# An attention output projection in three rounded products instead of one float32 product, and one turn later in TensorE's order

## The reference

```python
q = (x @ Wq + bq).reshape(B, N, H, d).transpose(0, 2, 1, 3)      # N = 164, H = 12, d = 16
k = (x @ Wk + bk).reshape(B, N, H, d).transpose(0, 2, 1, 3)
v = (x @ Wv + bv).reshape(B, N, H, d).transpose(0, 2, 1, 3)
scores = jnp.einsum('bhqd,bhkd->bhqk', q, k) * SCALE
allowed = jnp.abs(idx[:, None] - idx[None, :]) <= 64
attn = jax.nn.softmax(jnp.where(allowed[None, None], scores, -jnp.inf), axis=-1)
out = jnp.einsum('bhqk,bhkd->bhqd', attn, v).transpose(0, 2, 1, 3).reshape(B, N, D)
return out @ Wo + bo                                               # the product that is changed
```

## Time and profile before

| | us |
|---|---|
| median of 3 runs | 2368.55 |
| lowest, highest | 2356.19, 2369.52 |
| the profiled execution | 2377.01 |
| its span, first to last instruction | 2375.3 |
| TensorE busy | 2272.5 (96%) |
| VectorE busy | 1870.8 (79%) |
| ScalarE busy | 1412.7 (59%) |
| GpSimd busy | 297.8 (13%) |
| mean granted clock of TensorE | 0.98 |

### The profile page before, as it was taken

One profiled execution on the slowest core, in us unless ns is written; L12 is line 12 of the kernel. 1 busy time (PEld: TensorE's weight loads), 2 busy tenths in 40 slices (PEclk: granted clock), 3 DMA queues, 4 the chain that ended last, 5 costly groups with the idle time before them and its releaser, 6 DMA issues.

```text
span 2375.3 us, 49109 instructions
## 1 busy us (share of the span) xinstructions
PE 2272.5 (96%) x20033; PEld 2123.1 (89%) x20033; DVE 1870.8 (79%) x2241; ACT 1412.7 (59%) x1391; POOL 297.8 (13%) x169
## 2 busy tenths in 40 slices
PE   6599989999999889999999999999999999999999
PEld 5266778888888779999999999999999999999999
DVE  7599765666666578676676776679999999999996
ACT  6389403444444463543533534588998888888881
POOL 7522100000000013232232231000000000000000
PEclk9799998999999889999999999999999999999999
DMA  6555240111111101111111111120000000000000
GB/s 209 163 153 151 75 161 28 47 46 47 47 47 47 44 27 34 54 46 45 51 46 51 45 49 36 57 92 24 26 28 23 23 23 23 23 23 23 23 19 10
DMA packets 115454, 129.98 MB, mean 55 GB/s; under 512 B 17063, under 2 KB 106167, under 8 KB 115127
## 3 DMA queue, kind: packets, MB, share of 16 engines
q1 hardware_dynamic: 95215, 103.54, 14.5%
q10 hardware_dynamic: 16520, 14.34, 2.0%
q0 software_dynamic: 3616, 10.54, 1.7%
HBM read 92.79 MB, written 35.58 MB: 54 GB/s over the span
## 4 chain that ended last, share of the span: by engine, by line
PE 62%; DVE 2%; ACT 0%; issue 0%; DVEq 0%
PE spline_acc L1988 17%; PE spline_acc L1984 10%; PE spline_acc L1956 10%; PE spline_acc L1958 10%; PE spline_acc L1957 10%; PE spline_acc L1985 5%; PE spline_xT L764 0%; DVE spline_f L1726 0%; DVE spline_f_high L1726 0%; DVE spline_f_low L1726 0%; DVE spline_weights_split L1762 0%; DVE spline_b L1732 0%; DVE spline_front L1732 0%; DVE spline_f L1715 0%; DVE spline_front L803 0%; DVE spline_b L803 0%
## 5 line engine op out<-in xcount | busy, mean ns | idle before, releaser
L1956 PE MATMUL spline_acc<-spline_f,spline_weights_high 128*128 128x328 f32 x1536 | 483.2, 315 | 2.5 <-DVE spline_weights_low L1698 2.5
L1957 PE MATMUL spline_acc<-spline_f,spline_weights_high 128*128 128x328 f32 x1536 | 480.9, 313 | 0.0
L1958 PE MATMUL spline_acc<-spline_f,spline_weights_low 128*128 128x328 f32 x1536 | 480.6, 313 | 0.0
L1988 PE MATMUL spline_acc<-spline_weights,spline_f 128*128 128x192 f32 x1968 | 342.5, 327 | 0.0
L1988 PEld LDWEIGHTS spline_acc<-spline_weights,spline_f 128*128 128x128 f32 x1968 | 316.6, 190 | 0.0
L1984 PE MATMUL spline_acc<-spline_weights_split,spline_f_high 128*128 128x384 f32 x984 | 304.9, 374 | 2.1 <-DVE spline_f L1726 2.1
L1956 PEld LDWEIGHTS spline_acc<-spline_f,spline_weights_high 128*128 128x128 f32 x1536 | 289.1, 188 | 2.8 <-DVE spline_weights_low L1698 2.8
L1958 PEld LDWEIGHTS spline_acc<-spline_f,spline_weights_low 128*128 128x128 f32 x1536 | 290.2, 189 | 0.0
L1957 PEld LDWEIGHTS spline_acc<-spline_f,spline_weights_high 128*128 128x128 f32 x1536 | 289.7, 189 | 0.0
L1985 PE MATMUL spline_acc<-spline_weights_split,spline_f_low 128*128 128x192 f32 x984 | 248.5, 253 | 0.0
L1715 DVE SCALAR_TENSOR_TENSOR spline_f<-spline_front 128x984 fp32r<-128x984 f32 x128 | 148.6, 1202 | 93.7 <-PE spline_acc L1958 88.3
(11 more groups left out here) (240 smaller groups left out, 4932.3 us busy)
## 6 DMA issues: line engine op xcount, KB each, us to landing
spline_front<-pos_scr SPq DMA_DIRECT2D x32, 540.0 KB, 4.3
hid_scr<-spline_hid SPq DMA_DIRECT2D x64, 164.0 KB, 1.8
spline_xn<-hid_scr SPq DMA_DIRECT2D x41, 256.0 KB, 3.1
attend_spread<-rec_scr SPq DMA_DIRECT2D x128, 61.5 KB, 2.2
pix_scr<-spline_front SPq DMA_DIRECT2D x32, 225.0 KB
spline_weights_raw<-w SPq DMA_DIRECT2D x1, 6144.0 KB, 21.6
spline_step_to<-w SPq DMA_DIRECT2D x36, 128.0 KB, 2.1
spline_step_from<-w SPq DMA_DIRECT2D x36, 128.0 KB, 2.1
```

The costliest lines, as they stand in the source:

```text
L1956: nc.tensor.matmul(z, high, x_high, start=start, stop=False)
L1957: nc.tensor.matmul(z, high, x_low, start=False, stop=False)
L1958: last = nc.tensor.matmul(z, low, x_high, start=False, stop=stop)
L1988: last = nc.tensor.matmul(z, rest[:, cols], w2[:, i, r - SETS, :], start=False, stop=stop)
```

## The change

- `project_out` becomes 18 matmuls in F32R: for each head group high x high, high x low, low x high, of the weighed sums (`oT_high`, `oT_low`) and the output weights (`wo_high`, `wo_low`).
- The weights are split once, ahead of pair 0: ScalarE rounds, VectorE subtracts, and TensorE waits for both (`wo_ready`). Raw `wo` is loaded into the buffer of a later result.
- VectorE forms the product of `weigh` twice, once rounded into `oT_high`, once in full over `mixed`. A new step, `low_o`, subtracts; it, and no longer `weigh`, tells TensorE that the sums are there (`weighed`). It stands in turn 0 behind the maximum and, in the second sequence, behind the layer norm's statistics.
- TensorE projects after turn 1 instead of turn 0, and VectorE's residual rows move to turn 1, too.
- `spread` and `oT_low` share memory, `rec` moves into a free part of another buffer.

```diff
@@ buffers @@
-        wo, wo_in = sb("attend_wo", [P, HG, D]), sem("attend_wo_in")
+        wo_high, wo_low = (sb(f"attend_wo_{k}", [P, HG, D], F32R) for k in ("high", "low"))
+        wo_in, wo_ready = sem("attend_wo_in"), sem("attend_wo_ready")
...
-        rec = [sb(f"attend_rec{i}", [P, PART]) for i in range(2)]
-        spread = [sb(f"attend_spread{i}", [P, SC]) for i in range(2)]
-        oT = [sb(f"attend_oT{i}", [P, HG, TOK]) for i in range(2)]
+        rec = [c.rows[:, i, 64:64 + PART] for i in range(2)]
+        spread, oT_low = share(nc, stack, [(f"attend_spread{i}", [P, SC], F32) for i in range(2)],
+                               [(f"attend_oT_low{i}", [P, HG, TOK], F32R) for i in range(2)])
+        oT_high = [sb(f"attend_oT_high{i}", [P, HG, TOK], F32R) for i in range(2)]
         h2 = [sb(f"attend_h{u}", [P, 4, D]) for u in range(2)]
+        wo = h2[1][:, 0:HG, :]
@@ VectorE @@
             def weigh(t, i):
 
                 dve.wait_ge(spread_in[i], 64 * t + 64)
-                nc.vector.tensor_tensor(oT[i][:].rearrange("p g n -> p (g n)"), mixed[i][:], spread[i][:],
-                                        ALU.mult).then_inc(weighed, 1)
+                nc.vector.tensor_tensor(oT_high[i][:].rearrange("p g n -> p (g n)"), mixed[i][:], spread[i][:],
+                                        ALU.mult).then_inc(weigh_step, 1)
+                nc.vector.tensor_tensor(mixed[i][:], mixed[i][:], spread[i][:], ALU.mult).then_inc(weigh_step, 1)
+
+            def low_o(t, i):
+
+                dve.wait_ge(weigh_step, 4 * t + 2 * i + 2)
+                nc.vector.tensor_tensor(oT_low[i][:].rearrange("p g n -> p (g n)"), mixed[i][:],
+                                        oT_high[i][:].bitcast(F32).rearrange("p g n -> p (g n)"),
+                                        ALU.subtract).then_inc(weighed, 1)
...
                         if q == 0 and not first:
+                            low_o(t - 1, i)
+                        if q == 1 and not first:
                             residual(tt - 1 if u == 0 else tt, v, i, use(t, (Y_LAST if last else Y)[i]))
...
             norm_out(0, 1, start(START["X"][1]))
+            dve.wait_ge(wo_ready, 1)
+            nc.vector.tensor_tensor(wo_low[:], wo, wo_high[:].bitcast(F32), ALU.subtract).then_inc(wo_ready, 1)
             pair(0, 0, first=True)
...
             weigh(PAIRS - 1, 0)
+            low_o(PAIRS - 1, 0)
...
             weigh(PAIRS - 1, 1)
+            low_o(PAIRS - 1, 1)
@@ ScalarE @@
             high(mh[:], start(START["MAX"]))
+            act.wait_ge(wo_in, 16)
+            nc.scalar.activation(wo_high[:], wo, ACT.Copy).then_inc(wo_ready, 1)
             pair(0, 0, first=True)
@@ TensorE @@
                     for g in range(HG):
-                        last = nc.tensor.matmul(xb[0:ROWS, bank, n * D:(n + 1) * D],
-                                                oT[i][:, g, n * ROWS:(n + 1) * ROWS],
-                                                wo[:, g, :], start=(g == 0), stop=(g == HG - 1))
+                        y, cols = xb[0:ROWS, bank, n * D:(n + 1) * D], slice(n * ROWS, (n + 1) * ROWS)
+                        nc.tensor.matmul(y, oT_high[i][:, g, cols], wo_high[:, g, :], start=(g == 0), stop=False)
+                        nc.tensor.matmul(y, oT_high[i][:, g, cols], wo_low[:, g, :], start=False, stop=False)
+                        last = nc.tensor.matmul(y, oT_low[i][:, g, cols], wo_high[:, g, :], start=False,
+                                                stop=(g == HG - 1))
...
-                        if q == 0 and not first:
+                        if q == 1 and not first:
                             project_out(a - 2, i, use(t, Y[i]))
...
-            pe.wait_ge(wo_in, 16)
+            pe.wait_ge(wo_ready, 2)
             pair(0, 0, first=True)
```

More of the change, by code:

```diff
@@ L873, in attend_phase @@
         mix_ready, inverted, weighed = sem("attend_mix_ready"), sem("attend_inverted"), sem("attend_weighed")
+        weigh_step = sem("attend_weigh_step")
         h_ready = sem("attend_h_ready")
@@ L923, in _ @@
                 load(sp, x[u], x_in[u], u)
-            sp.dma_start(wo[:], a["wo"]).then_inc(wo_in, 16)
+            sp.dma_start(wo, a["wo"]).then_inc(wo_in, 16)
             sp.dma_start(w_raw[:], a["w1"].rearrange("p i (h r) o -> p (i h) (r o)", h=2)).then_inc(w1_in, 16)
```

## The result

The changed kernel took **2510.48 us** (median of 4 runs, 2485 to 2515) against 2367.11 before (4 runs, 2356 to 2370): **1.0587** times, 95% interval 1.0549 to 1.0625. The profiled execution took 2506.89 us, its span was 2505.2 at a mean granted clock of 0.939; before these were 2375.3 and 0.98. I predicted 2550 in a range of 2415 to 2625.

The account below looks back on a forecast made before the run. TensorE sets the attention loop's pace. New waits, start and end add 58 us to the profiled 2377.0, 2426 against the median; clock falls add 128, giving 2554, stated as 2550, range 2415 to 2625.

Parts of the forecast that it names:

- The projection as cover: In turn 0 the projection lies over VectorE's 1.07 us maximum, which turn 1's scores need; moved, it no longer covers it.
- The four waits: TensorE's new idle: first sequence 1.25 us before turn 1, 0.45 at transposes; second 0.75 before turn 1, 1.6 before projection.
- The projection at 1.76: 18 rounded matmuls take 1.76 us, scaled from ten in 1.05; some 0.25 less on average, 8 us in 32 sequences.
- The rival that its weight loads show: In the projection no weight load hides: 4 us more in 31 places, 2550 us; chance 0.02.
- Start and end: Before the loop TensorE waits for the split output weights, +4.9, taken as 7; the last two sequences add 2.4 us.
- The clock: TensorE's clock falls to 1.2 GHz in the loop's new waits, one and a half falls a pair: 128 us.
- They still land in time: Loads of the spread reciprocals still arrive before VectorE's product, though second product and reciprocal are 0.6 us late at most.

Follow-up runs that it names:

- with fillers: The changed kernel with dense filler work in TensorE's new waits, before turn 1 of both sequences and before the second one's projection: 2433.82 us, 1.0305.
- the subtraction ahead of the statistics: The changed kernel with VectorE's subtraction in the second sequence moved ahead of the layer norm statistics: 2472.73 us, 1.0466.
- the split alone: The changed kernel with projection and residual rows back in turn 0, the subtraction right behind the two products: 2459.76 us, 1.0416.
- the order alone: The kernel before with only projection and residual rows moved to turn 1, float32 products, no split: 2425.89 us, 1.0261.
- the kernel with the products between the keys: The changed kernel, projection back in turn 0, VectorE's products moved earlier into gaps, the second sequence's around the keys' remainders: 2372.43 us, 1.0015.

## Why the prediction was right, and its mis-sized term

- **The projection as cover**: right. With the cover gone, turn 1 waits for the maximum in both sequences, also with the arithmetic left as it was.
- **The four waits**: predicted 1.25 and 0.45 in the first sequence, 0.75 and 1.6 in the second; measured, on average over the 14 pairs, 1.25 and 0.46, 0.59 and 1.59. The pair at full clock: 32.58 predicted, 32.66 with fillers.
- **The projection at 1.76**: 1.73. Two of the ten matmuls that I scaled it from use 66 rows and not 128, and there are 32 projections and not 31; neither matters. The rival that its weight loads show is out: 18 matmuls of 128 rows, each with its own weights, take 0.1 us each. The rule of the Trainium skill (TensorE: Matmul & The Clock Gate, Part 3: Packing small matmuls) does not hold for these 18.
- **Start and end**: +7 and +2.4 predicted, and right in kind. From the transposed maxima ahead of pair 0 to its turn 1 TensorE took 15.1 us (358.52 to 373.62) instead of 7.1 (364.28 to 371.37), +8.0: 4.9 of them are the wait for the split weights (6.47) in place of the one for the maximum (1.56), as I had it, and most of the rest is a fall of the clock that began in it (0.50 from 362.3 to 372.3). From the last pair's turn 0 to the first product with the spline weights it took 59.0 us (934.36 to 993.38) instead of 54.4 (810.20 to 864.56), +4.7, where 1.34 for that sequence and 2.4 make 3.7.

```profile
365.30 1.12 PE L1384 MATMUL scores_by_key<-attend_q,attend_k 32*82 32x146 f32 x24 [6.47 <-DVE attend_wo_low L1153]
```

- **The clock**: the forecast was right and its size was not. I put one and a half falls of 13.5 us in each pair, 20 us at 1.2 GHz for 0.43 each, 128 us in all. Measured: 26 falls in 14 pairs, 14.0 us a pair (195.6 / 14), and 5.2 us a pair for them (37.86 less 32.66), 0.37 each: 73 us. More falls than I took, 1.9 a pair, but short, 7.5 us each: my 13.5 came from a fall in pair 0, and there is no row in the trace before of one in the middle of the loop. So the two errors partly cancel. That 55 us is nearly all that the sum was too high by on the profiled execution (2377 + 58 + 128 = 2563, measured 2507); that the rest cancels is luck, as the phases ahead of attention ended 5.8 us sooner in this execution than in that of the kernel before (358.52 against 364.28), with the same matmuls ahead of that point, which lies between 346 and 364 over the profiled kernels. I also thought that a shorter projection would bring the clock back later; most falls ended sooner. Why two lasted 44 us is open.
- **"They still land in time"**, of the spread reciprocals: true of this kernel, which shows no such wait, but only because its other waits made room (with the fillers VectorE waited for the broadcast in 4 first sequences, 3.0 us). It was the next thing to come late, and I gave it one sentence. My expectations for the two kernels that removed waits failed by it: by 28 us for the subtraction ahead of the statistics, and by 75 for the split alone, there in part by a plain miscount of VectorE's steps.

The shares: the order alone cost 61 us, the split in the old places 95, both 143; they don't add up. With the products in VectorE's gaps and the projection where it was, the split costs nothing that can be measured.

## What to carry to other kernels

An instruction on the busiest engine can be the cover of another engine's step: before moving it, ask what runs over that step afterwards. Splitting an operand in two is cheap on the engine that multiplies and dear on the one that splits, unless the new steps stand in gaps where that engine waits anyway. And when waits are taken out one by one, list what lands with little slack next, small transfers behind large ones above all.

## What the runs showed of the hardware

- Waits of 0.6 to 1.6 us among score groups, which use 32 rows of the array, were followed by 1.2 GHz 26 times in 14 pairs; ahead of one such fall TensorE was busy for 14.79 of 16.8 us at 2.4 GHz (638.90 to 655.70). With fillers in the waits it stayed at 2.4 for 443 us. In the kernel with the products between the keys, waits of 1.33 and 1.88 us brought no fall.
- In this loop a fall cost some 0.37 us for each us at 1.2 GHz, by the difference between the kernels with and without the fillers (5.2 us for 14.0 in a pair).
- A request that ScalarE or SyncE hands over in 0.31 to 0.51 us took 1.4 to 4.3 when several large ones had gone ahead on its queue. ScalarE did nothing else meanwhile: its next piece of work began 4.25 us late.
- Transfers of 82 and 46 rows ran at some 45 GB/s in their tail; as 80 + 2 and 32 + 14 rows that tail was gone.
